# A register load of VectorE moved ahead of the wait that opens its group step

## The chip, the core and the metric

The kernel runs on one core of a Trainium2 chip. The metric is the device time of one execution in microseconds; several executions are timed and their median is given. One execution is also recorded by the hardware profiler, and everything called a row below comes from that one.

## What is computed

One layer of a graph network on 6250 nodes and 106250 edges, sorted by their target node, with 256 features each:

```python
h = jnp.maximum(_layernorm(x, axis=-1), 0.0)
eq = h @ Wq + bq
ek = h @ Wk + bk
e = efeat @ We + be
m = jax.nn.relu(eq[dst] + ek[src] + e)
ft = jax.ops.segment_sum(m, dst, num_segments=n_nodes)
return x + ft @ Wr + br
```

## The kernel before

The program has three stages: node tables (`k_table`, `q_table`) are computed and stored to HBM; then the edges are worked through; then `ft` is multiplied by `Wr` and written out. The change lies in the middle stage, which is most of the time.

The edges are cut into 208 groups of 512, in 52 bodies of four groups (UNROLL = 4; the place of a group in its body is its slot, 0 to 3). The first and the last body are written out, the 50 between are the iterations of one hardware loop on each engine. Every engine has its own program for a group, and they meet in semaphores:

- GpSimd (`gather`, L487 to L498) waits for the indices and issues four indirect DMAs that bring 512 rows of `k_table` into `k_rows`. Each raises `s_wrote` by one when its descriptors are written and `s_rows` when its data is there. 16 gathers make one body.
- TensorE multiplies the edge features by `We` into PSUM `p_edge`, adds the picked rows of the q window (`edge_product`), sums messages into a window of 48 nodes (`window_sum`) and transposes that sum into `p_turn` (`turn_part`).
- ScalarE copies the indices, rounds edge features and messages to their high parts (`edge_hi`, `m_hi`) and makes the selection matrix.
- VectorE runs per group, in this order: `add_rows` (L838: `p_edge` += `k_rows`), `make_send` (L826: `send`, a comparison of two SBUF tensors), `add_sum` for the group three before (L859: `ft` += `p_turn` on the 48 nodes of that group), `edge_low` for the group two ahead (L818: `edge_lo` from `edge` and `edge_hi`, both in SBUF), and `message_low` (L846: `m_lo` from `p_edge` and `m_hi`).

`add_rows` opens the step with three waits. The first is on `s_wrote`: it holds VectorE until GpSimd has written the descriptors of all gathers of this group and the next (LEAD = 2). The others are on the edge product and on the arrived rows.

The nodes that a group touches begin at a number that is only known at run time. It stands in the table `win_tab` in SBUF. `add_sum` reads it with `value_load` (L852), which the sequencer of VectorE carries out: register arithmetic for the address (FUSED_REGOPS, ALU_OP), a TENSOR_LOAD from SBUF into a register, arithmetic, and a bounds assert (SEQ_ASSERT). The sequencer runs ahead of the engine: it hands over an instruction when its waits are met, and goes on to the next while the engine executes. Its own instructions are shown under the engine's name with a q (DVEq) and aren't counted as busy.

Of the kernel before, what the change touches and what calls it, by code (L numbers as in the profile page):

```python
# [60 lines left out]
def gnn_program(nc, x, dst_groups, dst_lanes, src_lanes, edges, Wq, bq, Wk, bk, We, be, Wr, br, out):  # L61
# [16 lines left out]
    with ctx:  # L78
# [155 lines left out]
        def after(eng, semaphore, n):  # L234


            if isinstance(n, int) and n < 0:
                return
            eng.wait_ge(semaphore, n + 1)
# [11 lines left out]
        def visit(it, u):  # L251

            body, slot = it + u // UNROLL, u % UNROLL
            return body, slot, body * UNROLL + slot, body // BODIES, body % BODIES

        def window_start(eng, w, ps):
            return nc.s_assert_within(eng.snap(w + ps * WIN), 0, ROWS - WIN, skip_runtime_bounds_check_because=(
                "either there is one pass, or the window table is all zeros"))

        def passes_of(eng):  # L260

            eng.wait_ge(s_tab, 1)
            return eng.value_load(more_passes[0:1, 0:1], min_val=0, max_val=PASSES - 1) * BODIES + BODIES
# [9 lines left out]
        def _(sp):  # L273
# [39 lines left out]
            def load_edge(it, u):  # L313
                body, slot, n, _, gb = visit(it, u)

                after(sp, s_ehi, n - 4)
                after(sp, s_elo, n - 4)
                g = gb * UNROLL + slot
                src = edges[g] if isinstance(g, int) else edges[bass.ds(g, 1)].rearrange("a p h e -> (a p) h e")
                sp.dma_start(edge[:, slot], src).then_inc(s_edge[slot], 16)  # L320
# [21 lines left out]
            def load_row(it, u):  # L342
                body, slot, n, _, gb = visit(it, u)

                after(sp, s_pick, n - 4)
                g = gb * UNROLL + slot
                sp.dma_start(rel_row[:, slot, :], rel_table[bass.ds(g, 1), :].to_broadcast([2 * WIN, GROUP]))\
                    .then_inc(s_row[slot], 16)
# [65 lines left out]
        def _(pool):  # L414
# [72 lines left out]
            def gather(it, u):  # L487
                _, slot, n, _, _ = visit(it, u)

                after(pool, s_idx, n)  # L490
                after(pool, s_pre, n - 4)
                pool.sem_inc(s_go, 1)
                for j in range(TILES):
                    nc.gpsimd.indirect_dma_start(  # L494
                        out=k_rows[:, slot, j, :], out_offset=None, in_=k_table,
                        in_offset=bass.IndirectOffsetOnAxis(ap=idx[:, slot, j:j + 1], axis=0),
                        engine_sem=s_wrote,
                    ).then_inc(s_rows[slot], 16)  # L498
# [169 lines left out]
        def _(dve):  # L668
# [144 lines left out]
            def edge_low(it, u):  # L813
                body, slot, n, _, _ = visit(it, u)

                after(dve, s_ehi, n)
                after(dve, s_prod, n - 2)
                nc.vector.tensor_tensor(edge_lo[:, slot % 2], edge[:, slot], edge_hi[:, slot % 2].bitcast(F32),  # L818
                                        ALU.subtract).then_inc(s_elo, 1)

            def make_send(it, u):
                body, slot, n, ps, gb = visit(it, u)

                after(dve, s_sum, n - 2)
                rel = rel_idx[:, bass.ds(gb * UNROLL + slot, 1), :].rearrange("p a t -> p (a t)")
                nc.vector.tensor_tensor(  # L826
                    send[:, slot % 2, :, 0:WIN], rel.unsqueeze(2).to_broadcast([LANES, TILES, WIN]),
                    window_cols[:, bass.ds(ps * WIN, WIN)].unsqueeze(1).to_broadcast([LANES, TILES, WIN]),
                    ALU.is_equal).then_inc(s_send, 1)

            def add_rows(it, u, last=False):
                body, slot, n, _, _ = visit(it, u)

                if not (last and u + LEAD >= UNROLL + 1):
                    dve.wait_ge(s_wrote, TILES * (n + LEAD))
                after(dve, s_prod, n)
                dve.wait_ge(s_rows[slot], 16 * TILES * (body + 1))
                nc.vector.tensor_tensor(p_edge[:, slot % 2, :], p_edge[:, slot % 2, :],  # L838
                                        k_rows[:, slot].rearrange("p t d -> p (t d)"), ALU.add).then_inc(s_pre, 1)

            def message_low(it, u):
                _, slot, n, _, _ = visit(it, u)

                after(dve, s_mhi, n)
                after(dve, s_sum, n - 2)
                nc.vector.scalar_tensor_tensor(m_lo[:, slot % 2, :], p_edge[:, slot % 2, :], 0.0,  # L846
                                               m_hi[:, slot % 2, :].bitcast(F32), ALU.max, ALU.subtract)\
                    .then_inc(s_mlo, 1)

            def add_sum(it, u):  # L850
                _, slot, n, ps, gb = visit(it, u)
                w = dve.value_load(win_tab[0:1, bass.ds(gb * UNROLL + slot, 1)], min_val=0, max_val=NODES - WIN)  # L852
                w0 = window_start(dve, w, ps)

                after(dve, s_turn, n)
                after(dve, s_ft, n - 1)
                window = ft[:, :, bass.ds(w0, WIN)]
                turned = p_turn[:, slot % 2, 0:D].rearrange("p (h n) -> p h n", h=HALVES)[:, :, 0:WIN]
                nc.vector.tensor_tensor(window, window, turned, ALU.add).then_inc(s_ft, 1)  # L859

            def steps(it, first=False, last=False):
                for u in range(UNROLL):
                    add_rows(it, u, last)
                    make_send(it, u)
                    if not (first and u < 3):
                        add_sum(it, u - 3)
                    if not (last and u + 2 >= UNROLL):
                        edge_low(it, u + 2)
                    message_low(it, u)
# [8 lines left out]
            dve.wait_ge(s_cleared, BLOCKS // 2)  # L878
            bodies = passes_of(dve)
            steps(0, first=True)  # L880
            with dve.Fori(1, bodies - 1) as it:
                steps(it)
            steps(bodies - 1, last=True)
            for u in range(UNROLL - 3, UNROLL):
                add_sum(bodies - 1, u)

            def ft_low(b, u):

# [202 lines left out]
```

## Time and profile before

| what | value |
|---|---|
| median of 3 runs | 1266.79 us (1265.26 to 1268.88) |
| the profiled execution: time | 1262.52 us |
| the profiled execution: span, first to last instruction | 1260.6 us |
| TensorE (PE) busy | 1118.6 us, 89% |
| VectorE (DVE) busy | 965.9 us, 77% |
| ScalarE (ACT) busy | 856.9 us, 68% |
| GpSimd (POOL) busy | 906.2 us, 72% |
| chain that ended last, by engine | POOL 28%, PE 25%, issue 22%, DVE 12%, DMA 6%, DVEq 3% |

The busy shares are averages over the span; the gaps between the instructions of one engine aren't in them. "issue" is time in which an engine waited for nothing that the profile shows.

### The profile page before, as it was taken

To read this page: it belongs to the slowest core of one execution; us is meant where nothing else is said; L and a number is where in the kernel's file an instruction comes from. 1 tells how busy PE (TensorE), PEld (TensorE's weight loads), DVE (VectorE), ACT (ScalarE), POOL (GpSimd) and SP (SyncE) were. 2 spreads that over 40 slices of the span, in tenths; PEclk is the share of its full clock that TensorE was granted. 3 is DMA by queue.
4 is the path that set the end of the run, shared out by engine and by line. 5 is a ranking of instruction groups with operands and counts; after the bars stand their busy time and mean duration, and the time that the engine had idled before them with its cause. 6 is when DMAs were issued, how large, how long until landed. Compare 5 with 4: busy or idle time off the path is not lost.

```text
span 1260.6 us, 33341 instructions
## 1 busy us (share of the span) xinstructions
PE 1118.6 (89%) x8632; PEld 1049.9 (83%) x8632; DVE 965.9 (77%) x1324; ACT 856.9 (68%) x1463; POOL 906.2 (72%) x946
## 2 busy tenths in 40 slices
PE   2997799999999999999999999999999999999876
PEld 1775788888888888888888888888888888888875
DVE  6886677777777777777777777777777777777788
ACT  2775577777777777777777777777777777777632
POOL 4545777777777777777777777777777777777653
PEclk9998999999999999999999999999999999999989
DMA  8887777777777777777777777777777777777664
GB/s 259 285 278 258 232 244 245 247 241 243 239 244 241 248 242 244 240 241 241 237 245 244 246 243 242 239 245 241 247 242 243 240 242 241 237 246 243 203 209 143
DMA packets 164469, 303.48 MB, mean 241 GB/s; under 512 B 29204, under 2 KB 110740, under 8 KB 164452
## 3 DMA queue, kind: packets, MB, share of 16 engines
q1 hardware_dynamic: 124516, 194.18, 47.5%
q0 software_dynamic: 39936, 109.11, 29.3%
q8 instruction: 6, 0.10, 0.0%
q14 instruction: 11, 0.09, 0.0%
HBM read 275.69 MB, written 27.48 MB: 240 GB/s over the span
## 4 chain that ended last, share of the span: by engine, by line
POOL 28%; PE 25%; issue 22%; DVE 12%; DMA 6%; DVEq 3%; ACT 2%; ACTq 0%; POOLq 0%; SPq 0%
POOL k_rows L494 28%; PE p_edge L929 14%; DVE m_lo L846 5%; PE p_sum L929 4%; DMA k_rows<-k_table,idx 4%; PE p_sum L1007 4%; DVE edge_lo L818 3%; DVEq L852 2%; PE p_edge L984 2%; DVE hT_lo L891 1%; DMA ft<-in_x 1%; DVE ft L859 1%; PE p_turn L938 1%; ACT idx L586 1%; DVE p_edge L838 1%
## 5 line engine op out<-in xcount | busy, mean ns | idle before, releaser
L494 POOL DMA_INDIRECT k_rows<-k_table,idx x832 | 817.8, 983 | 256.0 <-issue 240.1
L929 PE MATMUL p_edge<-we_hi,edge_hi 128*128 128x256 f32 x1664 | 487.0, 293 | 94.4 <-DVE m_lo L846 79.4
L929 PE MATMUL p_edge<-we_lo,edge_hi 128*128 128x256 f32 x1664 | 465.5, 280 | 0.0
L929 PE MATMUL p_edge<-we_hi,edge_lo 128*128 128x256 f32 x1664 | 465.1, 280 | 0.0
L838 DVE TENSOR_TENSOR p_edge<-p_edge,k_rows 128x1024 f32<-128x1024 f32 x208 | 256.4, 1233 | 244.9 <-DMA k_rows<-k_table,idx 244.8
L929 PEld LDWEIGHTS p_edge<-we_hi,edge_hi 128*128 128x128 f32 x1664 | 314.4, 189 | 140.7 <-issue 75.3
L615 ACT ACTIVATE m_hi<-p_edge 128x1024 fp32r<-128x1024 f32 x208 | 213.7, 1027 | 281.1 <-DVE p_edge L838 281.1
L929 PEld LDWEIGHTS p_edge<-we_lo,edge_hi 128*128 128x128 f32 x1664 | 315.2, 189 | 0.0
L929 PEld LDWEIGHTS p_edge<-we_hi,edge_lo 128*128 128x128 f32 x1664 | 313.2, 188 | 0.0
L818 DVE TENSOR_TENSOR edge_lo<-edge,edge_hi 128x1024 fp32r<-128x1024 f32 x208 | 253.9, 1221 | 0.9 <-ACT edge_hi L594 0.9
L846 DVE SCALAR_TENSOR_TENSOR m_lo<-p_edge,m_hi 128x1024 fp32r<-128x1024 f32 x208 | 253.2, 1217 | 1.3 <-ACT m_hi L615 1.3
L984 PE MATMUL p_edge<-q_win,pick 96*128 96x256 f32 x832 | 236.3, 284 | 0.0
L594 ACT ACTIVATE edge_hi<-edge 128x1024 fp32r<-128x1024 f32 x208 | 220.3, 1060 | 4.5 <-PE p_edge L984 4.5
L1007 PE MATMUL p_sum<-m_hi,send 128*128 128x256 f32 x832 | 208.8, 283 | 0.8 <-DVE m_lo L846 0.7
L1007 PE MATMUL p_sum<-m_lo,send 128*128 128x256 f32 x832 | 208.6, 283 | 0.0
L1007 PEld LDWEIGHTS p_sum<-m_hi,send 128*128 128x128 f32 x832 | 157.6, 189 | 1.2 <-issue 1.2
L1007 PEld LDWEIGHTS p_sum<-m_lo,send 128*128 128x128 f32 x832 | 157.5, 189 | 0.0
L984 PEld LDWEIGHTS p_edge<-q_win,pick 96*128 96x128 f32 x832 | 156.2, 188 | 0.0
L604 ACT ACTIVATE gap<-rel_row,lane_node 96x512 int16<-96x512 int16 x208 | 147.3, 708 | 3.1 <-DMA rel_row<-rel_table 3.0
L607 ACT ACTIVATE pick<-gap 96x512 fp32r<-96x512 int16 x208 | 131.5, 632 | 6.6
L622 ACT ACTIVATE sum_rows<-p_sum 128x256 f32<-128x256 f32 x208 | 78.5, 377 | 10.6 <-PE p_sum L1007 4.6
L994 PE MATMUL p_turn<-ident,sum_rows 128*128 128x128 f32 x416 | 79.9, 274 | 1.6 <-ACT sum_rows L622 1.6
(81 smaller groups left out, 931.3 us busy)
## 6 DMA issues: line engine op xcount, KB each, us to landing
edge<-in_edges SPq DMA_DIRECT2D x208, 512.0 KB, 3.8
rel_row<-rel_table SPq DMA_DIRECT2D x208, 96.0 KB
q_win<-q_table SPq DMA_DIRECT2D x416, 48.0 KB
q_table<-m_hi SPq DMA_DIRECT2D x52, 256.0 KB, 2.6
k_rows<-k_table,idx POOLq DMA_INDIRECT x832
ft<-in_x SPq DMA_DIRECT2D x4, 1664.0 KB, 11.9
k_table<-k_rows SPq DMA_DIRECT2D x52, 128.0 KB, 3.0
out_rows<-k_rows SPq DMA_DIRECT2D x13, 512.0 KB, 3.0
```

The lines of the kernel that those rows point to most:

```text
L494: nc.gpsimd.indirect_dma_start(out=k_rows[:, slot, j, :], out_offset=None, in_=k_table, in_offset=bass.IndirectOffsetOnAxis(ap=idx[:, slot ...
L594: nc.scalar.activation(edge_hi[:, slot % 2], edge[:, slot], ACT.Copy).then_inc(s_ehi, 1)
L604: nc.scalar.activation(gap[:], rel_row[:, slot, :], ACT.Abs, scale=-1.0, bias=lane_node[:, bass.ds(ps, 1)]).then_inc(s_gap, 1)
L607: nc.scalar.activation(pick[:, slot % 2, :], gap[:], ACT.Relu, bias=1.0, scale=-1.0)\
L615: nc.scalar.activation(m_hi[:, slot % 2, :], p_edge[:, slot % 2, :], ACT.Relu).then_inc(s_mhi, 1)
L818: nc.vector.tensor_tensor(edge_lo[:, slot % 2], edge[:, slot], edge_hi[:, slot % 2].bitcast(F32), ALU.subtract).then_inc(s_elo, 1)
L838: nc.vector.tensor_tensor(p_edge[:, slot % 2, :], p_edge[:, slot % 2, :], k_rows[:, slot].rearrange("p t d -> p (t d)"), ALU.add).then_inc ...
L846: nc.vector.scalar_tensor_tensor(m_lo[:, slot % 2, :], p_edge[:, slot % 2, :], 0.0, m_hi[:, slot % 2, :].bitcast(F32), ALU.max, ALU.subtract)\
L929: ins = nc.tensor.matmul(target, a(h), b[:, h, :], start=(h == 0 and n == 0), stop=(stop and h == HALVES - 1 and n == 2))
L984: ins = nc.tensor.matmul(target, pick[:, slot % 2, tile], q_win[:, slot, :], start=False, stop=True)
L994: ins = nc.tensor.transpose(p_turn[:, slot % 2, h * LANES:(h + 1) * LANES], sum_rows[:, slot % 2, h * LANES:(h + 1) * LANES], ident[:])
L1007: ins = nc.tensor.matmul(p_sum[:, slot % 2, 0:D], send[:, slot % 2, j, :], m[:, slot % 2, j * D:(j + 1) * D], start=(j == 0 and m is m_hi) ...
```

## The change

The load and its arithmetic become a function of their own, `window_of`, and `add_sum` gets the register. In the group step the function is called first, ahead of `add_rows` and its waits. In the tail behind the last body it stays where it was.

```diff
-            def add_sum(it, u):
-                _, slot, n, ps, gb = visit(it, u)
+            def window_of(it, u):
+                _, slot, _, ps, gb = visit(it, u)
                 w = dve.value_load(win_tab[0:1, bass.ds(gb * UNROLL + slot, 1)], min_val=0, max_val=NODES - WIN)
-                w0 = window_start(dve, w, ps)
+                return window_start(dve, w, ps)
+
+            def add_sum(it, u, w0):
+                _, slot, n, _, _ = visit(it, u)
 
                 after(dve, s_turn, n)
                 after(dve, s_ft, n - 1)
...
             def steps(it, first=False, last=False):
                 for u in range(UNROLL):
+                    if not (first and u < 3):
+                        w0 = window_of(it, u - 3)
                     add_rows(it, u, last)
                     make_send(it, u)
                     if not (first and u < 3):
-                        add_sum(it, u - 3)
+                        add_sum(it, u - 3, w0)
...
             for u in range(UNROLL - 3, UNROLL):
-                add_sum(bodies - 1, u)
+                add_sum(bodies - 1, u, window_of(bodies - 1, u))
```

## Rows read from the trace of the kernel before

**Rows 1.** The page's first line.

```profile
span 1260.6 us, 33341 instructions
```

**Rows 2.** Work on `k_rows` by stretch: span, DVE, ACT, POOL busy (count), PEclk, DMA, GB/s.

```profile
150.50:1181.00 1030.50, 247.80 (x201) 0.00 (x0) 785.95 (x802) 1.00 0.78 242
```

**Rows 3.** GpSimd's timeline, slots 3 and 0: start, duration, instruction, idle time before and releaser.

```profile
597.97 0.96 POOL L494 DMA_INDIRECT k_rows<-k_table,idx  x1 [0.30 <-issue]
...
600.49 0.95 POOL L494 DMA_INDIRECT k_rows<-k_table,idx  x1 [0.30 <-issue]
601.74 0.96 POOL L494 DMA_INDIRECT k_rows<-k_table,idx  x1 [0.30 <-issue]
603.00 0.95 POOL L494 DMA_INDIRECT k_rows<-k_table,idx  x1 [0.30 <-issue]
...
605.51 0.98 POOL L494 DMA_INDIRECT k_rows<-k_table,idx  x1 [0.30 <-issue]
606.80 1.36 POOL L494 DMA_INDIRECT k_rows<-k_table,idx  x1 [0.30 <-issue]
608.47 0.95 POOL L494 DMA_INDIRECT k_rows<-k_table,idx  x1 [0.30 <-ACT idx L586]
```

**Rows 4.** VectorE's timeline, the group with slot 3, and the same slot a body later.

```profile
598.96 1.23 DVE L838 TENSOR_TENSOR p_edge<-p_edge,k_rows 128x1024 f32<-128x1024 f32 x1 [1.11 <-DMA k_rows<-k_table,idx]
600.10 0.35 DVE L826 TENSOR_TENSOR send<-rel_idx,window_cols 128x192 fp32r x1
...
600.53 1.22 DVE L818 TENSOR_TENSOR edge_lo<-edge,edge_hi 128x1024 fp32r<-128x1024 f32 x1
601.67 1.22 DVE L846 SCALAR_TENSOR_TENSOR m_lo<-p_edge,m_hi 128x1024 fp32r<-128x1024 f32 x1
...
619.52 1.23 DVE L838 TENSOR_TENSOR p_edge<-p_edge,k_rows 128x1024 f32<-128x1024 f32 x1 [1.11 <-DMA k_rows<-k_table,idx]
```

**Rows 5.** VectorE's timeline, the group with slot 0.

```profile
604.18 1.23 DVE L838 TENSOR_TENSOR p_edge<-p_edge,k_rows 128x1024 f32<-128x1024 f32 x1 [1.29 <-DMA k_rows<-k_table,idx]
605.32 0.35 DVE L826 TENSOR_TENSOR send<-rel_idx,window_cols 128x192 fp32r x1
605.93 0.25 DVE L859 TENSOR_TENSOR ft<-ft,p_turn 128x96 f32 x1 [0.26 <-issue]
606.11 1.23 DVE L818 TENSOR_TENSOR edge_lo<-edge,edge_hi 128x1024 fp32r<-128x1024 f32 x1
```

**Rows 6.** L852, L859 in slot 0 (ns min/median/max); L859's idle time, whole edge phase.

```profile
L852 DVEq FUSED_REGOPS  x2: 154/172/190, 604.7 to 605.2; - x2
L852 DVEq TENSOR_LOAD <-win_tab x1: 305/305/305, 604.9 to 604.9; - x1
...
L859 DVEq FUSED_REGOPS  x1: 211/211/211, 605.7 to 605.7; - x1
...
  issue: 13.1, 50
```

**Rows 7.** VectorE's and GpSimd's timelines in the first body.

```profile
136.08 1.22 DVE L818 TENSOR_TENSOR edge_lo<-edge,edge_hi 128x1024 fp32r<-128x1024 f32 x1
...
136.20 1.93 POOL L494 DMA_INDIRECT k_rows<-k_table,idx  x1 [0.30 <-issue]
```

**Rows 8.** The same timelines in the last body, slot 0.

```profile
1179.72 1.23 DVE L838 TENSOR_TENSOR p_edge<-p_edge,k_rows 128x1024 f32<-128x1024 f32 x1 [1.29 <-DMA k_rows<-k_table,idx]
...
1181.32 1.23 DVE L818 TENSOR_TENSOR edge_lo<-edge,edge_hi 128x1024 fp32r<-128x1024 f32 x1
...
1182.35 1.02 POOL L494 DMA_INDIRECT k_rows<-k_table,idx  x1 [0.30 <-issue]
```

**Rows 9.** VectorE's sequencer: loop end (L881); first instruction of later steps (L835).

```profile
L881 DVEq FUSED_REGOPS  x2: 71/76/80, 601.3 to 601.7; - x2
...
L835 DVEq ALU_OP  x2: 45/45/45, 606.6 to 611.8; - x2
```

**Rows 10.** TensorE's timeline, the first product of the next group.

```profile
608.53 0.38 PE L929 MATMUL p_edge<-we_hi,edge_hi 128*128 128x256 f32 x1 [0.79 <-DVE m_lo L846]
```

## The prediction

> **What bounds the kernel now.** I read the trace in this order: the span, the time that all gathers take in the edge phase, the timeline of GpSimd's queue over one body of four groups, VectorE's timeline over the same body, and VectorE's own sequencer around the step that the change moves.
>
> The profiled execution has a span of 1260.6 us [rows 1] and a time of 1262.52 us. In one stretch of 1030.5 us, 802 gather instructions hold GpSimd for 785.95 us [rows 2]. Each is followed by 0.30 us in which it waits for nothing that the profile shows [rows 3]. 802 x 0.30 = 241 us, and 785.95 + 241 = 1027 us: GpSimd is never free. The path that sets the end is its queue of gathers. Sixteen gathers make one body, and one body lasts 619.52 - 598.96 = 20.56 us [rows 4].
>
> Each gather takes 0.95 us, and two of the sixteen take more: the one at 605.51 takes 0.98 and the one at 606.80 takes 1.36 us [rows 3]. Over the stretch, 785.95 - 802 x 0.953 = 21.6 us, which is 50 bodies of 0.43 (0.41 + 0.03 less rounding) [rows 2]. So the stretched gathers come once in each of the 50 looped bodies, and they alone can be won back: 16 x (0.953 + 0.304) = 20.11 us is the floor of a body.
>
> **Why those gathers are stretched.** A reader should lay GpSimd's starts over VectorE's. In the group with slot 3, VectorE runs the row addition at 598.96, `send` at 600.10 to 600.45 and `edge_lo` at 600.53 to 601.75 [rows 4]. Gathers start at 600.49, between the two, and at 601.74, at the end of `edge_lo`, and neither is stretched [rows 3]. In the group with slot 0, `edge_lo` lasts from 606.11 to 607.34 [rows 5]; the gather starts inside it, at 606.80, and ends at 608.16, which is 0.82 us after `edge_lo` has ended [rows 3]. The gather at 605.51 starts inside `send` (605.32 to 605.67) and ends at 606.49, again 0.82 after it [rows 3, 5]. The same distance comes back at two other places with other phases: 136.20 + 1.93 = 138.13, 0.83 after the `edge_lo` that ends at 137.30 [rows 7], and 1182.35 + 1.02 = 1183.37, 0.82 after the one that ends at 1182.55 [rows 8]. I take from this: a gather that starts inside `send` or `edge_lo` (the two steps with both inputs in SBUF) ends no earlier than 0.82 us after that step. `m_lo`, which reads one input from PSUM, doesn't do this: it lasts from 601.67 to 602.89, and the gather from 601.74 to 602.70 has its usual length in it [rows 3, 4].
>
> The Trainium skill bears on this twice, in "SBUF — State Buffer", section "Who interferes with whom". It says that a VectorE instruction with two SBUF inputs contends with a GpSimd instruction that reads SBUF, and these rows look like that. But it also says that its own probe saw `tensor_tensor` leave a DMA written by GpSimd alone. By that sentence the stretch would have another cause and the change would win nothing; that is the rival "nothing moves" below, where the mechanism is told from rows.
>
> **The change part by part.** Per group it removes one register load, its address arithmetic and its bounds assert from the place behind `send`, and puts the same instructions ahead of the wait on `s_wrote`. No work on an engine's data path is added or removed, no DMA moves, no queue of SP or GpSimd is passed.
>
> *Removal, three groups of four (slots 1 to 3).* The sequencer does the load while the row addition (1.23 us) is still executing, and the addition to `ft` starts with no idle time. Removing it there is worth 0; what hides it is the addition, and without that cover the chain would cost some 0.6 us.
>
> *Removal, slot 0.* Here the sequencer is late. Behind the row addition (dispatched 604.18) it does the arithmetic for `send`, then for the load 154 ns, 305 ns for the load itself, 190 ns of arithmetic, and 211 ns for the addition to `ft` [rows 6]. The addition to `ft` starts at 605.93 after 0.26 us of idle [rows 5]; there are 50 such waits, 13.1 us together [rows 6]. Distances from the row addition say what that is worth: `edge_lo` starts at 606.11 - 604.18 = 1.93 us here and at 600.53 - 598.96 = 1.57 us in the other groups [rows 4, 5]. The load's part of the delay is 154 + 305 + 190 ns and more, over 0.65 us, and the delay is 0.36, so all of it goes and VectorE itself, with its queue full, is next. `edge_lo` then starts 0.34 to 0.36 us earlier and ends near 607.0 instead of 607.34. The gather of 606.80 ends 0.82 later, at 607.82 instead of 608.16: 0.34 us off each body. The last body, which has no loop registers to compute, already shows this case: its `edge_lo` starts 1.60 us after the addition and its gather takes 1.02 instead of 1.36 us [rows 8]. I take 0.34 from that row, over 0.36 from VectorE's, since it is the gather itself.
>
> *Addition in front.* In slot 0 the sequencer has finished the branch at the loop's end at about 601.8 [rows 9]; the moved chain is 154 + 305 + 190 ns plus the assert and gaps, some 0.78 us, so it is done at 602.6. The signal that it must precede is the end of the gather of 603.00, at 603.95 [rows 3]: 1.3 us of cover. In slot 1 the sequencer is free at 606.6 [rows 9], done by 607.4, and the signal comes at 608.47 + 0.95 = 609.42 [rows 3]: 2.0 us. Cost 0. No row shows the load with `edge_lo` executing and `m_lo` queued, as it will be. Below: 0, since nothing waits for it. Above: it waits until `m_lo` has left the engine (608.47); it would then be done at 609.2, still ahead of 609.42. I take 0.
>
> *What is late next.* GpSimd again: a body of 20.56 - 0.34 = 20.22 us against its floor of 20.11. TensorE is no bound: before its product at 608.53 it has been idle for 0.79 us, for `m_lo` [rows 10], and this `m_lo` comes earlier by as much as the body is shortened.
>
> *Sum.* 50 bodies x 0.34 = 17.0 us. Against the profiled execution: 1262.52 - 17.0 = 1245.5 us. The median of the runs shown, 1266.79, is 4.3 above it; the same 17.0 off the median is 1249.8 us, and that is the forecast (-1.3%). By VectorE's rows (0.36) it would be 1248.8.
>
> **The rivals.**
>
> *The wait in slot 0 is shed too.* The row addition there starts 604.18 - 603.95 = 0.23 us after the signal, in the other groups 598.96 - 598.93 = 0.03 [rows 3 to 5], since two register instructions stand between its first wait and it. If moving the arithmetic makes these unnecessary, the last stretch of 0.10 us in each body goes as well: 5 us more, 1245. Nothing in the change aims at them.
>
> *Only the idle time comes back.* 50 x 0.26 = 13.1 us, 1253.7. For it: something of the arithmetic may stay behind `send`. Against it: the margin of 0.3 us worked out above.
>
> *Nothing moves.* The stretch is GpSimd's own, from the branch of its loop, and `edge_lo` only happens to end 0.82 before; VectorE's gain is then absorbed by the queue of gathers: 1266.8. For it: the stretch comes once in a body, as the branch does, and VectorE waits on the gathers in every group. Against it: 136.20, in another place of the body with another length (1.93), and 1182.35, both with the same 0.82.
>
> *Slower.* The front isn't covered. The mechanism has one place, the wait on `s_wrote`: whatever register work ends up between the gather's signal and the row addition pushes `send` and `edge_lo` later against the gathers. The rows give the price. In slots 1 to 3 `edge_lo` ends at 601.75; + 0.82 = 602.57, and the gather ends at 602.70 anyway, so 0.13 us of delay is free and all beyond it stretches every group's gathers. If the load's whole chain of 0.78 came behind the signal, 0.65 x 200 groups = 130 us; with 0.3 us behind it, 0.17 x 200 - 17 = +17 us, 1284. It decides from 0.2 us a group (0.07 x 200 = 14). For it: slot 0 already shows 0.2 us of such work. Against it: 1.3 and 2.0 us of cover.
>
> **How the numbers follow.** The forecast (1247 to 1252) 0.68; the wait shed too 0.08; idle time alone 0.09; nothing 0.08; slower 0.07. The measurement can tell about 0.3%, some 4 us, from no change. So faster 0.85, same 0.08, slower 0.07. The range takes in the first three: from 1245 less the 2 us that the runs scatter to 1253.7 plus the same, 1243 to 1256.
>
> **What would show it.** In the profile after: no idle time charged to issue before the addition to `ft`; `edge_lo` in slot 0 some 1.59 us after the row addition; the gathers of 1.36 us at 1.02; their sum over the stretch down by 17 us; a body of 20.2 us; the load's rows ahead of the row addition. The prediction is wrong if the gather stays at 1.36 although `edge_lo` came earlier, or if the row addition starts more than 0.03 us behind the gather's end in slots 1 to 3.

## The result, and the profile after

The changed kernel takes 1244.95 us (median of 4 runs, 1244.89 to 1247.33) against 1266.24 us (median of 4, 1265.26 to 1268.88) of the kernel before: a ratio of 0.9833, 95% interval 0.9814 to 0.9852. The forecast was 1249.8 us, the range 1243 to 1256. The profiled executions are 1244.89 us after and 1262.52 us before, 17.6 us apart. The median lies inside the range, but outside the 1247 to 1252 that the forecast itself claimed, and on the 1245 of the rival by which the wait in slot 0 is shed too. The time alone can't tell the two apart; the rows below can.

The page of the changed kernel, its first line, the chain that ended last by engine, and the line of the gathers (the page's columns: busy us, mean ns, idle time before):

```profile
span 1243.0 us, 33391 instructions
...
POOL 46%; issue 37%; PE 8%; DVE 3%; DMA 2%; ACT 1%; POOLq 1%; SPq 0%; DVEq 0%; ACTq 0%
...
L494 POOL DMA_INDIRECT k_rows<-k_table,idx x832 | 798.5, 960 | 256.0 <-issue 255.1
```

The chain is now GpSimd's queue almost alone: POOL and issue hold 83% of it, where they held 50%, and VectorE's sequencer (DVEq, 3% before, most of it the register load) has left it. In the page of before the same 832 gathers took 817.8 us with the same 256.0 us between them, so they take 19.3 us less. In the stretch of [rows 2], seen again, 812 gathers fit in where there were 802:

```profile
150.50:1181.00 1030.50, 251.50 (x204) 0.00 (x0) 778.86 (x812) 1.00 0.78 245
```

GpSimd's timeline of the changed kernel over the same place of a body, to be laid beside [rows 3]:

```profile
595.12 0.95 POOL L494 DMA_INDIRECT k_rows<-k_table,idx  x1 [0.30 <-issue]
596.38 0.95 POOL L494 DMA_INDIRECT k_rows<-k_table,idx  x1 [0.30 <-issue]
597.64 0.98 POOL L494 DMA_INDIRECT k_rows<-k_table,idx  x1 [0.30 <-issue]
598.92 1.00 POOL L494 DMA_INDIRECT k_rows<-k_table,idx  x1 [0.30 <-issue]
600.22 0.95 POOL L494 DMA_INDIRECT k_rows<-k_table,idx  x1 [0.30 <-issue]
```

And VectorE's, the group with slot 0, the row addition of slot 1 and that of slot 0 a body later, beside [rows 5]:

```profile
596.30 1.23 DVE L838 TENSOR_TENSOR p_edge<-p_edge,k_rows 128x1024 f32<-128x1024 f32 x1 [1.29 <-DMA k_rows<-k_table,idx]
597.45 0.35 DVE L826 TENSOR_TENSOR send<-rel_idx,window_cols 128x192 fp32r x1
597.71 0.25 DVE L862 TENSOR_TENSOR ft<-ft,p_turn 128x96 f32 x1
597.87 1.22 DVE L818 TENSOR_TENSOR edge_lo<-edge,edge_hi 128x1024 fp32r<-128x1024 f32 x1
...
601.21 1.23 DVE L838 TENSOR_TENSOR p_edge<-p_edge,k_rows 128x1024 f32<-128x1024 f32 x1 [0.98 <-DMA k_rows<-k_table,idx]
...
616.48 1.23 DVE L838 TENSOR_TENSOR p_edge<-p_edge,k_rows 128x1024 f32<-128x1024 f32 x1 [1.29 <-DMA k_rows<-k_table,idx]
```

The idle time before the addition to `ft` (now L862) is gone. `edge_lo` starts 597.87 - 596.30 = 1.57 us after the row addition instead of 1.93. The gather that overlaps it takes 1.00 us instead of 1.36 and ends at 599.92, 0.83 after `edge_lo` (599.09). A body lasts 616.48 - 596.30 = 20.18 us instead of 20.56. The load's rows in VectorE's sequencer, beside [rows 6] (kind, count, ns min/median/max, start), of slot 0 and, last, of slot 1:

```profile
L852 DVEq TENSOR_LOAD <-win_tab x1: 303/303/303, 594.1 to 594.1; - x1
...
L852 DVEq SEQ_ASSERT  x1: 23/23/23, 594.7 to 594.7; - x1
...
L852 DVEq TENSOR_LOAD <-win_tab x1: 303/303/303, 598.8 to 598.8; - x1
```

In slot 0 they are done at 594.7, while the `m_lo` that starts at 593.80 still executes; the gather that gives the signal ends at 595.12 + 0.95 = 596.07. 1.3 us of cover is left. In slot 1 the load runs at 598.8, while `edge_lo` (597.87 to 599.09) executes.

### The profile page after: what moved, and what is told of

Read it like the earlier page. It is cut to its first block, busy times and chain, and to the rows that moved or that the text cites. A ratio compares the mean times of both kernels' runs of the same rounds, so it can differ in the third digit from the quotient of the medians.

```text
span 1243.0 us, 33391 instructions
## 1 busy us (share of the span) xinstructions
PE 1119.0 (90%) x8632; PEld 1050.1 (84%) x8632; DVE 962.1 (77%) x1324; ACT 856.9 (69%) x1463; POOL 887.0 (71%) x946
## 4 chain that ended last, share of the span: by engine, by line
POOL 46%; issue 37%; PE 8%; DVE 3%; DMA 2%; ACT 1%; POOLq 1%; SPq 0%; DVEq 0%; ACTq 0%
POOL k_rows L494 46%; PE p_sum L934 5%; PE p_edge L934 3%; DVE hT_lo L896 1%; DMA ft<-in_x 1%; PE p_turn L943 1%; DMA k_rows<-k_table,idx 1%; POOLq L502 0%; DMA pre<-in_dst_groups 0%; DMA range_table<-top_g 0%; DVE k_rows L908 0%; DVE p_edge L838 0%; DVE k_rows L717 0%; POOLq L492 0%; DVE m_lo L846 0%
## 5 line engine op out<-in xcount | busy, mean ns | idle before, releaser
L494 POOL DMA_INDIRECT k_rows<-k_table,idx x832 | 798.5, 960 | 256.0 <-issue 255.1
L934 PEld LDWEIGHTS p_edge<-we_hi,edge_hi 128*128 128x128 f32 x1664 | 314.7, 189 | 121.0 <-issue 65.6
## 6 DMA issues: line engine op xcount, KB each, us to landing
q_table<-m_hi SPq DMA_DIRECT2D x52, 256.0 KB, 2.5
```

Source lines behind the costliest of these rows:

```text
L494: nc.gpsimd.indirect_dma_start(out=k_rows[:, slot, j, :], out_offset=None, in_=k_table, in_offset=bass.IndirectOffsetOnAxis(ap=idx[:, slot ...
L934: ins = nc.tensor.matmul(target, a(h), b[:, h, :], start=(h == 0 and n == 0), stop=(stop and h == HALVES - 1 and n == 2))
```

## The experiments

The theory: a gather that starts while VectorE executes `edge_lo` or `send` ends no earlier than 0.82 us after that step; the late load put `edge_lo` of slot 0 on a gather once in a body; the queue of gathers is the bound, so only stretched gathers cost time. The rivals: every load behind `send` costs; `m_lo` or the branch of GpSimd's loop stretches the gather; the late load costs through VectorE itself.

### A first series, on a chip where the gathers are not the bound

Four kernels ran first on a chip on which the kernel before takes 1611.35 us (25 runs), so its times can't be laid beside the others; its traces can.

```diff
# e1: in front in slot 0 alone; elsewhere behind send, as before (e2: the condition is u > 0)
-                    if not (first and u < 3):
+                    if not (first and u < 3) and u == 0:
                         w0 = window_of(it, u - 3)
...
-                        add_sum(it, u - 3, w0)
+                        add_sum(it, u - 3, w0 if u == 0 else window_of(it, u - 3))
```

> The load stands in front in slot 0 of each body alone; in slots 1 to 3 it stays behind send, as before the change. Theory (the late load in slot 0 pushes edge_lo into a gather): the whole gain, 1245 us, gathers of 1.00 us in slot 0, no idle time before the addition to ft. Rival (the gain comes from all loads that leave the place behind send): a quarter of it, 1261 us.

Measured: 1612.32 us, ratio 1.0001 (0.9984 to 1.0018).

> The counterpart: the load stands in front in slots 1 to 3 and behind send in slot 0. Theory: no gain, 1266 us, gathers of 1.36 us stay, 0.26 us of idle time before the addition to ft in 50 bodies. Rival (all loads count alike): three quarters of the gain, 1250 us.

Measured: 1614.17 us, ratio 1.0014 (1.0003 to 1.0026).

```diff
# e3: the kernel before, edge_lo from one SBUF input
-                nc.vector.tensor_tensor(edge_lo[:, slot % 2], edge[:, slot], edge_hi[:, slot % 2].bitcast(F32),
-                                        ALU.subtract).then_inc(s_elo, 1)
+                flat = lambda t: t.rearrange("p h e -> p (h e)")
+                nc.vector.tensor_reduce(flat(edge_lo[:, slot % 2]), flat(edge_hi[:, slot % 2]).bitcast(F32).unsqueeze(2),
+                                        axis=AX.X, op=ALU.max).then_inc(s_elo, 1)
```

> The kernel before, with edge_lo made by a reduction over one element, which reads one SBUF operand (edge_hi) instead of two; edge_lo is then a copy of edge_hi, so this part of the edge product is not computed. The load stays behind send and is late in slot 0. Theory (a step of VectorE with two SBUF inputs holds up a gather that starts inside it): the gather that takes 1.36 us takes 0.95 though edge_lo still overlaps it, 50 x 0.41 = 20.5 us less, 1246 us. Rivals (m_lo holds it up, or the branch of GpSimd's loop does): the gather stays at 1.36 us, 1266 us.

Measured: 1619.95 us, ratio 1.0053 (1.0033 to 1.0073).

```diff
# e4: the changed kernel, the wait on s_wrote last
-                if not (last and u + LEAD >= UNROLL + 1):
-                    dve.wait_ge(s_wrote, TILES * (n + LEAD))
                 after(dve, s_prod, n)
                 dve.wait_ge(s_rows[slot], 16 * TILES * (body + 1))
+                if not (last and u + LEAD >= UNROLL + 1):
+                    dve.wait_ge(s_wrote, TILES * (n + LEAD))
```

> The changed kernel, with the wait on s_wrote moved behind the other two waits of the row addition, so that in slot 0 the two register instructions that compute their thresholds run ahead of the signal. Theory: the row addition in slot 0 starts 0.03 us after the gather's end, as in the other slots, instead of 0.23; the last stretch of 0.04 + 0.03 us a body goes, 3.5 us less than the changed kernel, 1241.5 us. Rival (the 0.03 at the gather before it is the loop branch's own, and the row addition's start does not matter): within 1.5 us of the changed kernel.

Measured: 1614.39 us, ratio 1.0017 (1.0000 to 1.0035).

None of the four wins anything; e1, e3 and e4 were expected to win 20 us or more. One line of e1's list of waits (waiting engine, what it waited for, us in total, times, longest) says why; no such wait stands for the kernel before in its own trace, where GpSimd's gathers waited 240.1 us for nothing shown and 15.9 us for the indices:

```profile
POOL k_rows L494 <- DVE p_edge L838: 246.1, 95, 3.6
```

Here GpSimd stands still 246 us for a free buffer of `k_rows`. The chain that ended last gives it 1%. Where the gathers aren't the bound, shorter gathers win nothing. TensorE's mean granted clock is 0.90 in this trace and 0.99 in that of the kernel before. Sequencers are slower at times, too: a register instruction of SyncE (L347) that takes 37 ns at the median in both traces takes up to 732 ns here and at most 43 there. Why this chip is so much slower stays open.

But since the groups are irregular there, gathers start at many places of VectorE's step, which tests the rule itself. Counted over all rows of the timelines, in e1 161 gathers start inside `edge_lo` (more than 0.02 us after its start and 0.10 before its end), 146 of them are stretched, and all 146 end 0.82 to 0.84 us after it; the others start late in it, where 0.95 us reaches that point anyway. In e3 146 gathers start inside `edge_lo`, and none is stretched. The gathers of e1, then of e3, then the `edge_lo` of e3, whose length is as before (ns min/median/max, first and last start):

```profile
L494 POOL DMA_INDIRECT k_rows<-k_table,idx x832: 948/957/1974, 119.0 to 1530.9; - x167
```

```profile
L494 POOL DMA_INDIRECT k_rows<-k_table,idx x832: 947/953/1207, 120.6 to 1539.3; - x167
L819 DVE TENSOR_REDUCE edge_lo<-edge_hi x208: 1209/1220/1223, 118.1 to 1539.6; 128x1024 fp32r<-128x1024 f32 x104
```

The 1207 ns of e3 are the very first gather, which is as long in every kernel. What stretches a gather is thus `edge_lo` with its two SBUF inputs, not `m_lo` and not the branch. e3 also changes the instruction, from TENSOR_TENSOR to TENSOR_REDUCE, but the instruction alone doesn't do it: the row addition is a TENSOR_TENSOR of 1.23 us too, with one input in PSUM, and of the 206 gathers that start inside it in the trace of the kernel before none takes more than 0.97 us. Nor does any of the 152 that start inside `m_lo`.

### The same kernels where the gathers are the bound

> The kernel of e1 again, on another chip: there the kernel before took 1611 us and GpSimd's queue was no bound, so that the time could tell nothing. Expected as for e1 where the kernel before takes some 1266 us: the theory says the whole gain (ratio 0.983), the rival a quarter of it (0.996).

Measured: 1247.99 us against 1264.37 (7 runs), ratio 0.9869 (0.9853 to 0.9886), 16.4 us. That is nearly the forecast's 17, with one of four loads moved.

> The kernel of e2 again, where GpSimd's queue is the bound. Theory: no gain, ratio 1.000, gathers of 1.36 us and 0.26 us of idle time before the addition to ft in 50 bodies. Rival (all loads count alike): ratio 0.988.

Measured: 1266.15 us against 1265.64, ratio 0.9997 (0.9983 to 1.0011). Three of four loads moved win nothing. The idle time in slot 0 stays, `DVE ft L862 <- issue`, 50 times (waits, then the page's line of the gathers):

```profile
DVE ft L862 <- issue: 13.2, 50, 0.3
...
L494 POOL DMA_INDIRECT k_rows<-k_table,idx x832 | 817.5, 983 | 256.4 <-issue 240.3
```

> The kernel of e3 again (the kernel before, edge_lo a copy of edge_hi made with one SBUF input; this part of the edge product is not computed). In e3 no gather that started inside edge_lo was stretched. What is open is whether the time follows: theory, the load stays late in slot 0 and costs nothing, 50 x 0.41 = 20.5 us less than before and 2 more from the first bodies, ratio 0.982 to 0.984. Rival (the late load costs time by itself, through m_lo and TensorE): ratio 0.99 or more.

Measured: 1240.66 us against 1265.64, ratio 0.9799 (0.9779 to 0.9818), 25 us. The lower end of the expectation, 0.982, lies just above the interval. The kernel leaves the low part of the edge features out, so it answers the question and is no candidate. Slot 0 in its timelines:

```profile
592.19 1.23 DVE L839 TENSOR_TENSOR p_edge<-p_edge,k_rows 128x1024 f32<-128x1024 f32 x1 [1.30 <-DMA k_rows<-k_table,idx]
...
593.95 0.25 DVE L860 TENSOR_TENSOR ft<-ft,p_turn 128x96 f32 x1 [0.26 <-issue]
594.12 1.22 DVE L819 TENSOR_REDUCE edge_lo<-edge_hi 128x1024 fp32r<-128x1024 f32 x1
...
593.53 0.98 POOL L494 DMA_INDIRECT k_rows<-k_table,idx  x1 [0.30 <-issue]
594.82 0.96 POOL L494 DMA_INDIRECT k_rows<-k_table,idx  x1 [0.30 <-issue]
```

The load is as late as before the change: 0.26 us of idle time, `edge_lo` 1.93 us after the row addition. The gather at 594.82 starts inside `edge_lo` and takes 0.96 us. So the late load has no price of its own that these runs could tell; it costs through the gather. The one at 593.53, which starts inside `send`, is still stretched to 0.98.

### The dose

> The kernel of e4 again (changed kernel, wait on s_wrote last). Theory: 3.5 us less than the changed kernel, ratio to the kernel before 0.980 to 0.981, gathers in slot 0 at 0.95 us. Rival: no less than the changed kernel, 0.983.

Measured: 1241.33 us, ratio 0.9810 (0.9788 to 0.9832), 6.7 us less than e5, which in slot 0 is the changed kernel. The row addition in slot 0, `edge_lo` and three gathers:

```profile
593.04 1.23 DVE L838 TENSOR_TENSOR p_edge<-p_edge,k_rows 128x1024 f32<-128x1024 f32 x1 [1.10 <-DMA k_rows<-k_table,idx]
...
594.61 1.22 DVE L818 TENSOR_TENSOR edge_lo<-edge,edge_hi 128x1024 fp32r<-128x1024 f32 x1
...
592.05 0.96 POOL L494 DMA_INDIRECT k_rows<-k_table,idx  x1 [0.30 <-issue]
...
594.57 0.95 POOL L494 DMA_INDIRECT k_rows<-k_table,idx  x1 [0.30 <-issue]
595.83 0.95 POOL L494 DMA_INDIRECT k_rows<-k_table,idx  x1 [0.31 <-issue]
```

The threshold arithmetic of the row addition's last wait (L837), in the kernel before, where the signal comes at 603.95 [rows 3], and in e6:

```profile
L837 DVEq FUSED_REGOPS  x1: 53/53/53, 604.1 to 604.1; - x1
...
L837 DVEq FUSED_REGOPS  x1: 46/46/46, 591.8 to 591.8; - x1
```

This arithmetic stood behind the signal and now runs over a microsecond ahead of it. The row addition starts 593.04 - 593.01 = 0.03 us after the signal, and slot 0 now looks as [rows 4] do. No looped body holds a stretched gather. All gathers together take 793.2 us (799.4 in e5): 6.2 us, of which 3.5 are the looped bodies' 0.07 and 2.8 lie in the first 26 gathers, which the expectation had left out. There three gathers take 1.92 us in e5, and 0.95, 0.95 and 1.09 in e6; whether that is the moved wait's doing isn't shown. This is the fastest kernel here that leaves nothing out. It ran beside e5 and not beside the changed kernel itself.

> The kernel before, the load left behind send, with only the wait on s_wrote moved behind the other two. Theory (what counts is where edge_lo ends against the gather's start, whatever made it late): the row addition and with it edge_lo of slot 0 come 0.15 us earlier, the gather of 1.36 us takes 1.2 us, 50 x 0.15 = 7.7 us less, ratio 0.994. Rival (the register load is what costs): no change.

Measured: 1253.14 us against 1264.37, ratio 0.9907 (0.9891 to 0.9924), 11.2 us. The load is behind `send` and late as ever, and over half of the change's gain is there:

```profile
599.71 1.23 DVE L838 TENSOR_TENSOR p_edge<-p_edge,k_rows 128x1024 f32<-128x1024 f32 x1 [1.11 <-DMA k_rows<-k_table,idx]
...
601.46 0.25 DVE L859 TENSOR_TENSOR ft<-ft,p_turn 128x96 f32 x1 [0.26 <-issue]
601.64 1.23 DVE L818 TENSOR_TENSOR edge_lo<-edge,edge_hi 128x1024 fp32r<-128x1024 f32 x1
...
602.50 1.19 POOL L494 DMA_INDIRECT k_rows<-k_table,idx  x1 [0.30 <-issue]
```

The gather takes 1.19 us instead of 1.36, as expected (0.17 x 50 = 8.5 us); it ends 0.82 after `edge_lo` again. The gain is more than the 7.7 us of the expectation, whose ratio of 0.994 lies outside the interval. The gather before it also lost its 0.03, and the first body its long ones: the page's sum of all gathers is 806.2 instead of 817.8 us, 11.6 less.

```diff
# e8: the changed kernel, one more load between signal and row addition
+                if u > 0:
+                    dve.sem_inc(s_mark, 1)
+                    dve.value_load(more_passes[0:1, 0:1], min_val=0, max_val=PASSES - 1)
                 nc.vector.tensor_tensor(p_edge[:, slot % 2, :], p_edge[:, slot % 2, :],
```

> The changed kernel with one more register load in slots 1 to 3, between the signal and the row addition, its result unused. Theory: the row addition comes some 0.6 us after the signal instead of 0.03; 0.12 us of it is free, the rest stretches every such group, 0.5 x 156 = 78 us more than the changed kernel, some 1320 us. Rival (VectorE is idle over 1.1 us in every group, so 0.6 us more of register work costs nothing): 1245 us.

Measured: 1346.95 us, ratio 1.0651 (1.0633 to 1.0669). Slot 1:

```profile
643.66 0.95 POOL L495 DMA_INDIRECT k_rows<-k_table,idx  x1 [0.30 <-issue]
...
647.43 1.61 POOL L495 DMA_INDIRECT k_rows<-k_table,idx  x1 [0.30 <-issue]
...
L841 DVEq TENSOR_LOAD <-more_passes x1: 322/322/322, 644.8 to 644.8; - x1
...
645.43 1.23 DVE L842 TENSOR_TENSOR p_edge<-p_edge,k_rows 128x1024 f32<-128x1024 f32 x1 [1.76 <-DMA k_rows<-k_table,idx]
...
647.00 1.22 DVE L819 TENSOR_TENSOR edge_lo<-edge,edge_hi 128x1024 fp32r<-128x1024 f32 x1
```

The row addition starts 645.43 - 644.61 = 0.82 us after the signal, 0.79 later than in the other kernels; the expectation had 0.6 for it and so fell short by a quarter. The gather takes 1.61 us, 0.66 more than usual: 0.13 us were free, the rest one to one. 0.66 x 156 groups = 103 us; the page's sum of all gathers is 98 us above that of the changed kernel, and the median 102 us above the changed kernel's in the other series. VectorE has 1.76 us of idle time before this row addition, and it doesn't help.

### What the front can hold

```diff
# e11: two more loads in front of the waits (e12: range(6))
                         w0 = window_of(it, u - 3)
+                    for _ in range(2):
+                        dve.value_load(more_passes[0:1, 0:1], min_val=0, max_val=PASSES - 1)
                     add_rows(it, u, last)
```

> The changed kernel with two more register loads in front of every group's waits, results unused. e8's trace gives 0.62 us a load with its arithmetic, so the front grows by 1.25 us; the cover in slot 0 is 1.30 us (sequencer done 594.78, signal 596.08 in the trace of the changed kernel) and larger in the others. Theory: all of it is covered, within 2 us of the changed kernel, ratio 0.983 to 0.987. Rival (loads in front wait for the engine to run empty, or delay the row addition): over 10 us more.

Measured: 1248.01 us, ratio 0.9858 (0.9839 to 0.9877). That is 3.1 us above the changed kernel's median, from another series, where the expectation allowed 2. The gathers take 799.1 us in all against 798.5, and the first of them starts 1.2 us later: three loads in front cost what one does, as far as the traces can tell.

> The same with six more loads: 3.7 us, beyond any cover. Theory: VectorE's sequencer becomes the bound: 2.4 us from the row addition to the end of the group's last hand-over, 0.8 for its own chain and 3.7 for the six, some 6.9 us a group instead of 5.05, 208 x 1.85 = 385 us more, 1630 us. Rival (the sequencer's work in front is free): as two more.

Measured: 1675.23 us, ratio 1.3224 (1.3201 to 1.3246). The six loads in one group, two row additions in a row, the asserts of the six loads behind them, and the next row addition, in slot 0:

```profile
L869 DVEq TENSOR_LOAD <-more_passes x6: 303/304/305, 774.2 to 777.2; - x6
...
799.69 1.23 DVE L838 TENSOR_TENSOR p_edge<-p_edge,k_rows 128x1024 f32<-128x1024 f32 x1 [2.98 <-issue]
...
806.63 1.23 DVE L838 TENSOR_TENSOR p_edge<-p_edge,k_rows 128x1024 f32<-128x1024 f32 x1 [3.02 <-issue]
...
L869 DVEq SEQ_ASSERT  x6: 23/23/23, 810.8 to 813.9; - x6
...
814.26 1.23 DVE L838 TENSOR_TENSOR p_edge<-p_edge,k_rows 128x1024 f32<-128x1024 f32 x1 [3.70 <-DMA k_rows<-k_table,idx]
```

The first two are 6.94 us apart, as worked out (6.9), and the idle time is now charged to issue. The total is 45 us over the expected 1630. From slot 3 to slot 0 it takes 814.26 - 806.63 = 7.63 us, since VectorE's sequencer has the end of the loop to do there as well (L888, 809.0 to 809.5). The profile puts this wait down to the DMA of the rows, but the last assert starts only at 813.9, and the gathers that this row addition waits for had ended over 9 us before: the sequencer is last here too. Four groups of 6.9 us would be 27.6 us; a body lasts 814.26 - 785.68 = 28.58, and 50 x 0.98 = 49 us is about what the expectation missed. GpSimd is now the one that waits, 353 us for indices in all.

## Why the prediction was right

*The bound.* Right. In every kernel in which GpSimd isn't starved, the span is the sum of the gathers plus 443 to 447 us: 1260.6 - 817.8 = 443 before, 1243.0 - 798.5 = 445 after, 446 in e5, e6 and e11, 445 in e7, 447 in e8 and e9, 443 in e10. Part of the spread of 4 us is the start of the first gather, at 118.6 us before and between 118.6 and 121.0 in the others.

*What stretches a gather.* Right in each part: 0.82 us after `edge_lo` in e7 and e8 too, where it was put elsewhere; gone in e3 and e10 with the second SBUF input. The rule of the Trainium skill ("SBUF — State Buffer", "Who interferes with whom") that a VectorE instruction with two SBUF inputs contends with a GpSimd instruction that reads SBUF fits all of it. The sentence there by which `tensor_tensor` left a DMA written by GpSimd alone does not hold for these indirect gathers, whose indices lie in SBUF: 54 of 54 that started inside `edge_lo` were stretched in the trace of before. The measurement decides. That the indices are the read in question is argued, not shown.

*Slots 1 to 3 worth nothing, slot 0 worth all.* Right: e9 (0.9997) and e5 (0.9869).

*The size.* The term was 0.34 us a body, from the last body's gather [rows 8]; the looped bodies gave 1.36 - 1.00 = 0.36, the value of VectorE's rows. The step that chose between the two chose the worse one: in the last body `edge_lo` follows the row addition by 1.60 us, in the changed kernel by 1.57. 50 x 0.36 = 18 us, and the first body gave 1.0 more, which the sum didn't have and which is luck. It is one gather, shown here with VectorE's rows, before and after:

```profile
130.08 1.22 DVE L818 TENSOR_TENSOR edge_lo<-edge,edge_hi 128x1024 fp32r<-128x1024 f32 x1
130.22 1.92 POOL L494 DMA_INDIRECT k_rows<-k_table,idx  x1 [0.31 <-issue]
...
130.02 1.23 DVE L838 TENSOR_TENSOR p_edge<-p_edge,k_rows 128x1024 f32<-128x1024 f32 x1 [10.37 <-PE p_edge L989]
131.43 1.22 DVE L818 TENSOR_TENSOR edge_lo<-edge,edge_hi 128x1024 fp32r<-128x1024 f32 x1
131.38 0.96 POOL L494 DMA_INDIRECT k_rows<-k_table,idx  x1 [0.30 <-issue]
```

In the changed kernel the edge product came last there and held the row addition to 0.2 us after the gathers' signal, so `edge_lo` began 0.05 us after the gather instead of 0.14 before it. No load is moved in this step, and in e5 and e9 the gather takes 1.92 us as before. Of the 19 us the first gather, which started 1.2 us later than before (119.8 instead of 118.6), took one back; the profiled executions differ by 17.6 us.

*The median.* The 21.3 us between the medians are 3.7 more than between the profiled executions. The timed runs of the kernel before lay up to 6.4 us above its profiled one, those of the changed kernel at most 2.4. In the other two series the kernel before had medians of 1264.4 and 1265.6, and e5 gained 16.4. So 17 us describes the change better than 21. The forecast added 4.3 us, the distance of the median from the profiled execution, to the changed kernel as well; that was an assumption, and it failed, and this alone put the median on the rival's 1245. Its cause stays open.

*The front.* Right: 1.3 us of cover in slot 0, full use of it in e11, the bound turned over in e12. The load runs without harm while `edge_lo` executes and `m_lo` is still to start (598.8 in slot 1), which no row of before had shown.

*The slower rival.* Its price, one to one beyond 0.13 us, is what e8 measured. It did not occur since the row addition in slots 1 to 3 still starts 0.03 us after the signal (in slot 1, from rounded rows, 601.21 - (600.22 + 0.95) = 0.04). *The wait in slot 0* was not shed: the row addition there starts 0.23 us after the signal as before (596.30 - 596.07), and e6 shows what it would have brought.

## What to carry to other kernels

When one queue is the bound, lay its instructions over the other engines' timelines and ask which of them are longer than their kin, and what ends a constant time before they do; a late step on an idle engine may cost only by what it collides with. Register loads belong where the sequencer waits anyway, and that place has a capacity: measure it from the sequencer's last instruction to the signal. Of several waits, the one that comes last in time should be written last, with the arithmetic of the others' thresholds ahead of it.

## What the runs showed of the hardware

- An indirect gather of GpSimd takes 0.95 us, and one that starts inside a VectorE step with two SBUF inputs ends 0.82 us after that step (0.82 to 0.84 in 146 cases). A step of the same length with one SBUF input leaves it alone: as a reduction, 0 of 146 stretched; with the other input in PSUM, none of 206 above 0.97 us.
- A register load on VectorE's sequencer takes 0.30 us; with its arithmetic and assert, loads in a row start 0.61 us apart (six in e12). Three of them per group were hidden (e11), seven set the pace (e12).
- Waits that stand on register values can put the arithmetic of a later threshold behind an earlier wait: 0.23 us between the signal and the engine in slot 0, 0.03 in e6, where the thresholds were there beforehand.
- The kernel before had medians of 1264 to 1266 us in three series and of 1611 us in a fourth, on another chip, where the traces show a mean granted clock of 0.90 instead of 0.99.
